# A new order of row maxima, layer norm, POOL sums, squares and results in a software-pipelined attention and feed-forward kernel

## The reference

```
xn  = rms_norm(x, g_norm) * (1 + scale) + shift        # scale, shift from cond @ W_emb + b_emb
q,k,v = split(xn @ W_qkv);  q = rms_norm(q, g_q);  k = rms_norm(k, g_k)
o   = softmax(q @ k.T * 32**-0.5) @ v
y   = o + o @ W_out
h   = layer_norm(y) @ ternary(w_fc).T                  # absmax_quant falls out with the scales
h   = gelu(h)
out = x + layer_norm(h) @ ternary(w_proj).T
```

## Time and profile before

| | |
|---|---|
| median of 3 runs | 1229.25 us (1228.51 to 1229.79) |
| profiled execution, its own time | 1230.94 us |
| its span, first to last instruction | 1229.2 us |
| mean granted PE clock | 0.965 of full |
| PE busy | 1091.4 us, 89% of the span |
| DVE, ACT, POOL busy | 868.6, 800.2, 568.5 us |
| start of one iteration to the next, iterations 2 to 13 | 68.6 us |

### The profile page before, as it was taken

The page is one execution under the profiler, slowest core; times in us unless marked ns, Lnnn a source line. Parts: engine busy times, 40 slices in busy tenths (PEclk is TensorE's granted clock), DMA queues, the critical chain, the costliest instruction groups (busy, mean ns, idle before and its releaser), DMA issues. The chain is left out here.

```text
span 1229.2 us, 26312 instructions
## 1 busy us (share of the span) xinstructions
PE 1091.4 (89%) x9524; PEld 690.2 (56%) x9524; DVE 868.6 (71%) x1609; ACT 800.2 (65%) x1365; POOL 568.5 (46%) x370
## 2 busy tenths in 40 slices
PE   4726799999999899999999899999999899999687
PEld 4303365655656565665656565665656565656354
DVE  3485857778677777778676777778786777777444
ACT  2525477685858577685858586685858586675742
POOL 0534636190825436280826446280917345371515
PEclk9867889999999999999999999999999999999889
DMA  8251200213021210203030211103030211002001
GB/s 326 86 183 40 69 35 10 79 36 87 36 69 51 56 64 18 67 34 85 34 85 35 68 51 30 56 34 86 34 85 34 68 51 40 30 24 48 35 1 52
DMA packets 74445, 74.20 MB, mean 60 GB/s; under 512 B 6560, under 2 KB 55968, under 8 KB 73888
## 3 DMA queue, kind: packets, MB, share of 16 engines
q1 hardware_dynamic: 74400, 73.59, 19.6%
HBM read 39.89 MB, written 8.39 MB: 39 GB/s over the span
## 5 line engine op out<-in xcount | busy, mean ns | idle before, releaser
L786 PE MATMUL F<-yT_hi,fc_t 128*128 128x256 f16 x1024 | 227.8, 274 | 0.0
L787 PE MATMUL F<-yT_lo,fc_t 128*128 128x256 f16 x1024 | 227.4, 274 | 0.0
L555 POOL TENSOR_TENSOR rqk<-ssq,half 128x16 f32<-128x16 f32 x64 | 186.4, 2912 | 63.3 <-DVE ssq L1216 63.3
L627 PE MATMUL F<-proj_t,hs 128*128 128x512 f16 x512 | 197.3, 385 | 3.8 <-DVE hs L1183 3.8
L629 PE MATMUL F<-proj_t,hs 128*128 128x512 f16 x512 | 197.0, 385 | 0.0
L1183 DVE SCALAR_TENSOR_TENSOR hs<-hg,g_inv,hs 128x512 f16<-128x512 f32 x128 | 99.5, 777 | 82.4 <-ACT hs L906 80.8
L526 POOL TENSOR_TENSOR acc<-acc,hg 128x512 f32<-128x512 f32 x96 | 144.2, 1502 | 7.3
L526 POOL TENSOR_TENSOR acc<-hg 128x512 f32<-128x512 f32 x16 | 20.3, 1270 | 265.1 <-DVE hs L1183 256.4
L901 ACT ACTIVATE hg<-F,g_fc 128x512 f32<-128x512 f32 x128 | 87.9, 687 | 71.3 <-PE F L787 69.8
L533 POOL TENSOR_TENSOR acc<-acc,hq 128x512 f32<-128x512 f32 x96 | 123.2, 1283 | 19.1 <-ACT hq L962 8.7
L698 PE MATMUL PV<-v_hi,p_hi 128*128 128x33 f16 x1024 | 105.2, 179 | 30.0 <-DVE p_lo L1196 22.2
(11 more groups left out here) (188 smaller groups left out, 2784.5 us busy)
## 6 DMA issues: line engine op xcount, KB each, us to landing
stk<-qkT SPq DMA_DIRECT2D x128, 128.0 KB, 2.5
xtok<-in_x SPq DMA_DIRECT2D x16, 512.0 KB, 3.4
xT_sb<-in_xT SPq DMA_DIRECT2D x16, 512.0 KB, 3.2
stk<-qkT SPq DMA_DIRECT2D x128, 64.0 KB, 2.1
xres<-in_x SPq DMA_DIRECT2D x16, 512.0 KB, 3.2
out<-xres SPq DMA_DIRECT2D x16, 512.0 KB, 2.8
stk<-in_w_emb SPq DMA_DIRECT2D x1, 2048.0 KB, 7.9
proj_t<-in_w_fcT SPq DMA_DIRECT2D x2, 1024.0 KB, 12.5
```

The lines of the kernel that those rows point to most:

```text
L555: pool.tensor_tensor(rqk[:, n % 2, :], ssq[:, n % 2, :], half[:, :], ALU.pow).then_inc(rqk_r, 1)
L627: pe.matmul(FB[t][:, :], hs[:, 0, k // 2, col:col + P], proj_t[:, k, :], start=(k == 0), stop=False)
L786: pe.matmul(dst, w, yT_hi[:, k, :], start=(k == 0), stop=False)
L787: mm = pe.matmul(dst, w, yT_lo[:, k, :], start=False, stop=(k == KT - 1))
```

## The change

It changes orders; no arithmetic is added or removed. On PE, `group_max(1)` goes behind two of the `second` calls and `y_turn(0)`, and `group_max(3)` from behind unit 1 to behind unit 2. On DVE, `norm_stats(1)` goes ahead of the fourth maximum, maxima 4 and 5 go ahead of `y_lo(0)`, maximum 7 behind `y_lo(1)`; `input_lo` goes from ahead of `result(late, 0)` to unit 1, and maxima 12 to 15 from units 1 and 2 to units 2 and 3; in the slots `heads_out` goes ahead of `p_lo` and `heads_lo` ahead of the sum of squares; `result(ffn, 1)` and `residual(ffn, 1)` go from slot 14 to slot 15 and behind the last `heads_out`. On ACT, three of the squares go into units 2, 4 and 6, and the rest move (tile 3 to slot 2, tiles 4 and 5 one slot earlier). On POOL, the seven adds of gelu tiles start when three low parts are there and all stand ahead of the first power.

```diff
-MAX_BEFORE_LOW = [(8, 9, 10, 11), (12, 13), (14, 15), (), (), (), (), ()]
+MAX_BEFORE_LOW = [(8, 9, 10, 11), (), (12, 13), (14, 15), (), (), (), ()]
+INPUT_LOW_UNIT = 1
-FOLD_AT, RMS_AT, RS2_AT, STAT_AT, OUT1_AT = 11, 3, 12, 14, 14
-HSQ_AT = {1: (0,), 2: (1,), 3: (2,), 4: (3,), 5: (4,), 6: (5,), 8: (6,), 9: (7,)}
-SUMS_BEFORE = {0: [("h", n) for n in range(1, 6)], 7: [("h", 6), ("h", 7)] + [("q", n) for n in range(1, 5)],
+FOLD_AT, RMS_AT, RS2_AT, STAT_AT, OUT1_AT = 11, 3, 12, 14, 15
+HSQ_UNIT = {2: 0, 4: 1, 6: 2}
+HSQ_AT = {2: (3,), 4: (4,), 5: (5,), 8: (6,), 9: (7,)}
+SUMS_BEFORE = {0: [("h", n) for n in range(1, UNITS)], 7: [("q", n) for n in range(1, 5)],
                10: [("q", n) for n in range(5, 8)]}
-SUMS_AFTER_LOW = 5
+SUMS_AFTER_LOW = 3
@@ PE, first stage
-                if att is not None:
-                    group_max(1)
                 if late is not None:
                     second(late, 0, 2)
                     second(late, 0, 3)
                 if ffn is not None:
                     y_turn(0)
+                if att is not None:
+                    group_max(1)
@@ PE, units
-                    if att is not None and n == 1:
+                    if att is not None and n == 2:
                         group_max(3)
@@ ACT, units
                         if att is None:
                             square_hidden(ffn, n)
+                        elif n in HSQ_UNIT:
+                            square_hidden(ffn, HSQ_UNIT[n])
@@ DVE, first stage
                     norm_bias(ffn, 0)
+                    norm_stats(ffn, 1)
                 maxes((3,))
                 if ffn is not None:
-                    norm_stats(ffn, 1)
-                maxes((4,))
-                if ffn is not None:
                     norm_bias(ffn, 1)
-                maxes((5,))
+                maxes((4, 5))
                 if ffn is not None:
                     y_lo(i, ffn, 0)
-                maxes((6, 7))
+                maxes((6,))
                 if ffn is not None:
                     y_lo(i, ffn, 1)
-                if qkv is not None:
-                    for k in range(KT):
-                        input_lo(qkv, k)
+                maxes((7,))
                 if late is not None:
                     result(late, 0)
@@ DVE, units
                     maxes(MAX_BEFORE_LOW[n])
+                    if n == INPUT_LOW_UNIT and qkv is not None:
+                        for k in range(KT):
+                            input_lo(qkv, k)
@@ DVE, slots: heads_out(att, h // HPG - 1) now ahead of p_lo(h), for h = 5, 9, 13
@@ DVE, slots: heads_lo(att, n) now behind p_lo(h), ahead of the sum of squares and the norm
@@ DVE, end
                     if h == OUT1_AT and ffn is not None:
                         result(ffn, 1)
-                        residual(ffn, 1)
                 if att is not None:
                     heads_out(att, GROUPS - 1)
+                if ffn is not None:
+                    residual(ffn, 1)
```

More of the change, by code:

```diff
@@ L1190, in iteration @@
                 for h in range(HEADS):
+                    if att is not None and h % HPG == BEHIND - 1 and h > HPG:
+                        heads_out(att, h // HPG - 1)
                     if att is not None:
@@ L1208, in iteration @@
                         dve.wait_ge(s_cs, 2)
-                    if att is not None and h % HPG == BEHIND - 1 and h > HPG:
-                        heads_out(att, h // HPG - 1)
+                    kind, n = TURN_AT.get(h, (None, 0))
+                    if kind == "heads" and att is not None:
+                        heads_lo(att, n)
                     if qkv is not None and h in square_at(qkv):
@@ L1241, in iteration @@
                                                      ALU.mult, ALU.mult).then_inc(u_r if k < KT - 1 else unturned, 1)
-                    if kind == "heads" and att is not None:
-                        heads_lo(att, n)
                     if kind == "stats" and ffn is not None:
```

## The result

The changed kernel takes 1188.74 us in the median of 4 runs (1188.35 to 1189.64), against 1229.35 of the kernel before in 4 runs: a ratio of 0.9671, 95% interval 0.9656 to 0.9687. The forecast was 1188. The span of the profiled execution is 1186.6 us.

A forecast was written before the change was run, and what follows sets the result against it. The prediction took PE's work plus its waits to bound the kernel: 2.7 us saved per iteration, 13 x 2.7 = 35.1, plus 2.25 in iteration 1 and 3.5 at the ends, sum 41, giving 1188 us; range 1180 to 1204.

The forecast's parts named there:

- PE bounds the kernel: Loop iteration: PE's own work plus its waits set the length; reordering can give back at most about 4.15 of 68.63 us.
- First stage: PE at group_max(1): its wait for the fourth row maximum goes and group_max(2) fits with 0.2 to spare, gaining 0.75 us.
- Second stage: Transpose of the maxima: a new wait of 0.3 to 0.7 us leaves 0.45 of the front gain; bounds 1.15 and -0.5.
- Squares on ACT: Three squares among the units: PE doesn't wait for gelu, first exp about 0.2 late; costed at nothing, at most 0.6 us.
- The sum of 2.7: Gain per iteration: 0.45 + 0.2 + 0.35 + 0.6 + 1.1 = 2.7 us, from 68.6 to 65.9.
- POOL, "worth nothing by itself, but is what lets the rest pass": Adds moved ahead of the first power: piece 3 ready about 1.4 us earlier; otherwise 0 to 1.6 us lost there.
- The holds beside the adds: Low parts beside POOL's adds: one hold absorbed by DVE's idle time; rival of 0.6 us per iteration, 1196, chance 0.09.
- Slots, 1.15: Waits of 0.35 and 0.2 for heads_out and 0.6 at piece 2's transpose go, by moving heads_out and heads_lo forward.
- End, 1.1: Ahead of values(15): p_lo(15) no longer stands behind result and residual, so 1.1 of the 1.55 us wait go.
- The sum over the ends of the pipeline, 3.5: Iterations 0 and 15: earlier heads_out and p_lo(15), with the front of iteration 15, give some 3.5 us.

The follow-up runs named there:

- front_only: The kernel before with only the edits of the first two stages (order of group_max, layer norm, maxima, input_lo, result): 1224.21 us against 1229.5.
- squares_back: The changed kernel with all of ACT's squares in the slots, as in the kernel before: 1191.82 us.
- pool_back: The changed kernel with POOL's adds as before, starting behind five low parts and split between the first and third powers: 1199.21 us.
- short_adds: The changed kernel with each of POOL's adds of gelu tiles cut to 2 of 512 columns: 1189.94 us.
- maxima_early: The changed kernel with group_max(3) behind unit 1, maxima 12 to 15 in units 1 and 2 again, and input_lo in unit 3: 1201.78 us.

## Why the prediction was right, step by step

- **PE bounds the kernel, and the waits are all there is to gain.** Right. The iteration lost 68.63 - 65.95 = 2.68 us against 2.7 forecast, and PE's work in it stayed what it was. From start to start three waits are left, 0.60, 0.55 and 0.42. The list of the prediction lacked one that its text on the second stage names, 0.17 ahead of `group_max(3)`; it has gone too.
- **First stage, 0.75 gained.** Right: no wait at `group_max(1)`, `group_max(2)` without one too. From the last product of `o @ W_out` to `group_max(2)` PE took 573.05 - 565.43 = 7.62 us before and 556.00 - 549.15 = 6.85 after, 0.77 less. The eighth maximum started at 555.08 in the trace after; it ended at 555.76 and PE began the group at 556.00, the 0.2 to spare of the sum.
- **Second stage pays back all but 0.45.** Right in mechanism and nearly in size: a wait of 0.43 recorded (0.60 from start to start, forecast 0.3 to 0.7) at the transpose of the maxima, and 0.37 per iteration in `front_only`, where the forecast was 0.45.
- **Squares on ACT, a cost of nothing.** Right for what they cost in the units, but they are worth 0.24 us per iteration (`squares_back`), for which the prediction had no term. I had looked for what the squares do in the units and hadn't asked what their leaving does in the slots once PE is earlier. The sum of 2.7 holds because it has no wait at the rms transpose, which it owes to this edit without saying so.
- **POOL, "worth nothing by itself, but is what lets the rest pass".** The second half is right: without it 0.59 us per iteration are lost (`pool_back`), within the 0 to 1.6 given. The first half wasn't run, since no kernel has POOL's new order alone. The place was wrong: piece 2 and the statistics transpose, not piece 3. And the two adds that leave the front of slot 7's power were read as up to 3.4 us; in the trace before they take 2.62.
- **The holds beside the adds, absorbed.** Right for the changed kernel (`short_adds`: no gain), by a few hundredths of a microsecond as estimated there. The 0.6 per iteration given if they weren't absorbed was too low for a neighbouring order: 1.24 in `maxima_early`. The reading behind it was incomplete: the prediction took the low part's 0.74 from before the adds began, and three low parts already ran beside adds in the kernel before, without being held (the last section shows why). The Trainium skill's sentence (GPSIMD Engine Reference, Key points) names the pairs that collide, and the traces agree in three kinds of instruction with two SBUF inputs beside adds: the low part 0.74 to 1.75, the residual 0.74 to 1.75, `input_lo` 1.66 to 4.71 for four. The fourth kind, the fold beside POOL's power, was not held.
- **Slots, 1.15.** Right only with the other two edits. Alone, slots and end give 1.42 in place of 2.25: two places that weren't waits before become waits, and at piece 2 0.37 of the 0.60 stay. In the changed kernel none of the three is left.
- **End, 1.1.** Right: 1.14 alone.
- **The sum over the ends of the pipeline, 3.5.** Of the 40.6 us gained, 14 x 2.68 = 37.5 are the loop's. The 3.1 left fit it, though the start by itself varies by 2 us between kernels and I didn't take it apart; here luck may have a part.

The parts don't add up by themselves: 5.3 (first stages) and 23.4 (slots and end) make 28.7 of 40.6. The other 12 appear when POOL's and ACT's orders are changed too: per iteration 0.37 + 1.42 + 0.59 + 0.24 = 2.62 of the 2.68. The forecast came out right as it was worked out for all edits at once.

## What to carry to other kernels

When one engine is full and waits for another a few tenths of a microsecond at a time, list its waits over one iteration, and for each ask what stands ahead of the releasing instruction in its engine's order; the sum of the waits bounds the gain. Then move everything behind a removed wait forward by it and look again at what had shown no wait: here three transposes would have come 0.2 to 0.4 us too early, and it is why two edits that were not aimed at any wait of the kernel before, POOL's and ACT's orders, cost 10.5 and 3.1 us when they were undone. Keep DVE instructions with two SBUF inputs away from POOL's adds where DVE has no idle time before a deadline; where it waits anyway, the overlap is free.

## What the runs showed of the hardware

DVE instructions with two SBUF inputs are held beside POOL's elementwise adds by up to one add each: four of 0.48 us each took 4.71 us together, one of 0.74 took 1.75. Which of the two waits goes by which started first. In the kernel before a low part started 0.29 us ahead of an add (586.67 in the earlier trace rows) and kept its length; the adds took 1.69 on average there, 1.27 alone. In `front_only`, with POOL's rule unchanged, a low part started 0.31 us behind an add and took 1.51. The timelines of DVE in the kernel before, and of DVE and POOL in `front_only`:

```profile
586.38 0.76 DVE L1183 SCALAR_TENSOR_TENSOR hs<-hg,g_inv,hs 128x512 f16<-128x512 f32 x1 [1.21 <-ACT hs L906]
```

```profile
583.31 1.51 DVE L1183 SCALAR_TENSOR_TENSOR hs<-hg,g_inv,hs 128x512 f16<-128x512 f32 x1 [1.81 <-ACT hs L907]
583.00 6.30 POOL L527 TENSOR_TENSOR acc<-acc,hg 128x512 f32<-128x512 f32 x4
```

So a small shift in order changes DVE's busy time with the work unchanged: 51.69 us per iteration before, 53.62 in `front_only`, 54.24 after.

DVE instructions with one input in PSUM beside such adds kept their 0.68 to 0.69, and the fold of the sums (two SBUF inputs) beside POOL's power took 0.68; all 16 folds of the kernel before took 0.68 to 0.69. So the adds held such instructions, and this power did not. In the kernel before:

```profile
602.40 0.69 DVE L1196 TENSOR_TENSOR p_lo<-SB,p_hi 128x512 f16<-128x512 f32 x1 [0.48 <-ACT p_hi L928]
616.41 0.68 DVE L1258 TENSOR_TENSOR accf<-acc 128x512 f32<-128x512 f32 x1
```

```profile
601.20 2.62 POOL L526 TENSOR_TENSOR acc<-acc,hg 128x512 f32<-128x512 f32 x2
616.18 2.91 POOL L555 TENSOR_TENSOR rqk<-ssq,half 128x16 f32<-128x16 f32 x1
```
